# A four-layer hybrid network in one program: where a gated output lives in PSUM, and how the expert stages begin and end

## The reference

```python
# layer 0: deformable convolution (8 groups, 9 taps), batch norm as a scale and a shift, and a gate
out = (acc * mask[..., None]).sum(axis=3).reshape(N, P, C) @ w_out + b_out
out = out * inv + (bn_beta - bn_mean * inv)
x = x + out * sigmoid(out)
# layer 1: a scan layer;  layer 2: attention by cosines, then experts
t = t + experts_2(layernorm(t))
# layer 3: additive attention, then experts
t = t + attention_3(layernorm(t))
t = t + experts_3(layernorm(t))
x = t.transpose(0, 2, 1).reshape(x.shape)          # back to channels

def experts(x):                                    # both expert layers
    probs = softmax(x @ router_w + router_b)
    top_p, top_i = top_k(probs, 2);  top_p = top_p / sum(top_p)
    out = einsum("bnd,edc->bnec", x, expert_w) + expert_b      # 8 experts
    return sum over the two chosen experts of top_p * out
```

## Time and profile before

| what | value |
| --- | --- |
| median of 3 runs | 8086.49 us (8081.16 to 8256.99) |
| profiled execution, its own time | 8087.35 us |
| its span | 8085.6 us |
| busy: TensorE, VectorE, ScalarE, GpSimd | 6444.7, 6521.0, 5476.0, 2058.6 us |
| mean granted clock of TensorE | 0.921 of 2.4 GHz |
| deformable layer | to about 1881 us |
| expert stage L2 | 3518 to about 3826 us |
| expert stage L3 and way out | 7964 to 8065, and 8065 to 8085.6 us |

### The profile page before, as it was taken

The page is one execution under the profiler, slowest core; times in us unless marked ns, Lnnn a source line. Parts: engine busy times, 40 slices in busy tenths (PEclk is TensorE's granted clock), DMA queues, the critical chain, the costliest instruction groups (busy, mean ns, idle before and its releaser), DMA issues. The chain is left out here.

```text
span 8085.6 us, 98492 instructions
## 1 busy us (share of the span) xinstructions
PE 6444.7 (80%) x36662; PEld 2250.5 (28%) x36662; DVE 6521.0 (81%) x12658; ACT 5476.0 (68%) x4096; POOL 2058.6 (25%) x1980
## 2 busy tenths in 40 slices
PE   7988898886888599989677776788767877778777
PEld 2222222222344234434221112222222222222223
DVE  7899899997675577758887778898888898888985
ACT  4223222222555455535899998999989999899995
POOL 5556665661000166546100000000000000000002
PEclk9999999987888799989899998999989999899998
DMA  1000000000100000000000000000000000000000
GB/s 51 1 1 1 1 1 1 1 1 15 28 23 24 8 1 1 1 3 1 6 1 1 1 1 1 1 1 1 1 11 1 1 1 1 11 1 1 1 1 24
DMA packets 19194, 46.19 MB, mean 6 GB/s; under 512 B 5786, under 2 KB 8604, under 8 KB 17566
## 3 DMA queue, kind: packets, MB, share of 16 engines
q1 hardware_dynamic: 18718, 39.86, 1.6%
HBM read 14.68 MB, written 8.39 MB: 3 GB/s over the span
## 5 line engine op out<-in xcount | busy, mean ns | idle before, releaser
L2440 ACT ACTIVATE aa_tanh<-aa_tanh 128x4096 f32<-128x4096 f32 (+8 forms) x1280 | 3686.9, 2963 | 117.9 <-DVE aa_tanh L2617 117.7
L2617 DVE TENSOR_SCALAR aa_tanh<-aa_f_times,aa_g_bias 128x1024 f32<-128x1024 f32 (+18 forms) x5120 | 2982.4, 646 | 593.2 <-PE aa_scores L2485 588.7
L2485 PE MATMUL aa_scores<-aa_tanh,aa_w_spread 128*32 128x512 f32 (+8 forms) x18432 | 2177.6, 587 | 827.1 <-ACT aa_tanh L2440 731.3
L2485 PEld LDWEIGHTS aa_scores<-aa_tanh,aa_w_spread 128*32 128x32 f32 x18432 | 583.5, 112 | 2257.0 <-ACT aa_tanh L2440 1051.1
L278 POOL TENSOR_TENSOR near_tap_weights<-near_hat_y_mask,near_hat_x 128x1024 f32<-128x1024 f32 x400 | 935.9, 2364 | 464.6 <-PE near_weights_spread L562 459.3
L562 PE MATMUL near_weights_spread<-near_tap_weights,near_spread_consts 36*64 36x512 f32 x6272 | 795.0, 626 | 164.2 <-DVE near_weighted L346 156.2
L576 PE MATMUL near_out_sum<-near_weighted,near_w_out 128*128 128x512 f32 x1408 | 735.4, 647 | 77.6 <-DVE near_weighted L357 76.6
L2499 PE MATMUL aa_out_sum<-aa_weights,aa_normed 128*128 128x512 f32 (+3 forms) x1152 | 649.7, 648 | 120.6 <-DVE aa_weights L2626 120.5
L2407 POOL TENSOR_SCALAR aa_group_normed<-x_rows,norm_scale,aa_shift_plus 128x128 f32<-128x128 f32 x96 | 75.3, 796 | 2453.2 <-PE aa_turned L2526 1780.5
L346 DVE TENSOR_TENSOR near_weights_spread<-near_weights_spread,near_values 128x1024 f32<-128x1024 f32 x432 | 529.1, 1225 | 86.2 <-PE near_weights_spread L562 81.3
L357 DVE TENSOR_TENSOR near_weighted<-near_weighted,near_weights_spread 128x1024 f32<-128x1024 f32 x432 | 527.3, 1221 | 20.8 <-DVE near_weights_spread L346 0.5
(11 more groups left out here) (355 smaller groups left out, 7230.5 us busy)
## 6 DMA issues: line engine op xcount, KB each, us to landing
l_taps<-l_scan_in_out SPq DMA_DIRECT2D x256, 64.0 KB, 2.0
x_rows<-in_x SPq DMA_DIRECT2D x4, 2048.0 KB, 14.7
out_x<-x_rows SPq DMA_DIRECT2D x4, 2048.0 KB, 6.3
qa_weights_in<-in_quantum SPq DMA_DIRECT2D x1, 1280.0 KB, 5.8
L_ffn_expert_w<-in_L_ffn_expert_w SPq DMA_DIRECT2D x2, 512.0 KB
near_spread_consts<-in_deform_consts SPq DMA_DIRECT2D x1, 805.5 KB, 7.7
l_weights<-in_mamba SPq DMA_DIRECT2D x1, 557.0 KB
consts_sb<-in_consts SPq DMA_DIRECT2D x1, 516.5 KB
```

The source lines that it names most:

```text
L2440: a.activation(TH[:, (4 * n + tt) % PLACES, 0:length], TH[:, (4 * n + tt) % PLACES, 0:length], ACT.Tanh).then_inc(th_ready, 1)
L2485: last = t.matmul(sp_[32 * q:32 * q + 32, n % 2, s:e], W2S[:, tt, :], TH[:, (4 * n + tt) % PLACES, o + s:o + e], start=tt == 0, stop=tt == ...
L2617: ins = v.tensor_scalar(TH[:, (4 * n + tt) % PLACES, at[q]:at[q] + w - s], FR[:, m % 2, lo + s:CHUNK], GB[:, key:key + 1], None, ALU.add)
```

## The change

1. **Deformable layer.** The gate writes its result back into `acc` in PSUM, and `YB` is no longer used for it. `add_out` reads `acc` and stands after shift 2 of the next block, not after shift 8. TensorE's first sum of the next block waits for that add (`x_done`) and no longer for the gate (`y_ready`); the gate waits for no add.
2. **Expert stages.** VectorE normalizes the first 16 tiles into a tile of its own (`UF`); GpSimd begins with the fifth group. TensorE turns the first four groups, then centres the router, makes all four groups of logits, and then centres the expert weights, which ScalarE copies out in two halves. Seven semaphores more are raised at the start of the stage.
3. **Weights kept.** `attention_and_experts` writes its centred weights to tiles that outlive it, and the last expert stage uses them: no loads and no centring there.
4. **Way out inside.** In the last expert stage finished tiles are turned back inside the loop (`turn_back`, `store_back`), seven groups of four after the tiles 17, 19, 21, 23, 25, 27 and 30 and the last after the loop, through the PSUM places of `turn`; ScalarE stores them and SP sends each group (256 KB) as it is stored. `to_channels` is gone.

```diff
@@ deform_near @@
-                v.tensor_tensor(x, x, YB[:, :, :], ALU.add).then_inc(x_done, 1)
+                v.tensor_tensor(x, x, acc[:, :, :], ALU.add).then_inc(x_done, 1)
...
-                    if U and t == 8:
+                    if U and t == 2:
                         add_out(U - 1)
...
             def bn_gate(U):
                 a.wait_ge(proj, 1 + (U + 1) * NGR)
-                if U:
-                    a.wait_ge(x_done, 1 + U)
-                a.activation(YB[:, :, :], acc[:, :, :], ACT.Silu, bias=BB[:, 0:1], scale=INV[:, 0:1]).then_inc(y_ready, 1)
+                a.activation(acc[:, :, :], acc[:, :, :], ACT.Silu, bias=BB[:, 0:1], scale=INV[:, 0:1]).then_inc(y_ready, 1)
...
                 if g == 0 and U:
-                    t.wait_ge(y_ready, 1 + U)
+                    t.wait_ge(x_done, 1 + U)
@@ moe_layer @@
+        if kept:
+            RWC, EWC = kept
...
+        backs = {}
+        if out is not None:
+            for g in range(NTL // 4 - 1):
+                backs[max(4 * g + 6, NTL - CK + 2 * g + 1)] = g
...
         @block.sync
+            if out is not None:
+                for g in range(NTL // 4):
+                    sp.wait_ge(stored, 1 + g + 1)
+                    sp.dma_start(out[:, g * BANK:(g + 1) * BANK], T[:, first * P + g * BANK:first * P + (g + 1) * BANK]).then_inc(sent, 16)
+                sp.wait_ge(sent, 1 + 16 * (NTL // 4))
+            if kept:
+                return
...
         @block.gpsimd
-            pool.memset(ON[:, :], 1.0 / P).then_inc(prep, 1)
-            pool.wait_ge(prep, 1 + 3)
-            for g in range(CG):
-                normalize(g)
+            if not kept:
+                pool.memset(ON[:, :], 1.0 / P).then_inc(prep, 1)
+            pool.wait_ge(sh_ready, 1 + 1)
...
         @block.tensor
+            def turn_back(g):
+                n = NTL // 4 + g
+                t_.wait_ge(t_ready, 1 + 4 * g + 4)
+                if g >= 2:
+                    t_.wait_ge(stored, 1 + g - 1)
+                for k in range(4):
+                    last = t_.transpose(up[:, n % 2, k * P:(k + 1) * P], tokens(4 * g + k), C["ident"])
+                last.then_inc(back, 1)
...
             for g in range(CG):
                 turn(g)
-                if g:
-                    logits(g - 1)
-            logits(CG - 1)
+            if not kept:
+                t_.wait_ge(loaded, 1 + 64)
+                t_.wait_ge(prep, 1 + 2)
...
+            for g in range(CG):
+                logits(g)
+            if not kept:
...
             for t in range(NTL):
...
+                if t in backs:
+                    turn_back(backs[t])
+            if out is not None:
+                turn_back(NTL // 4 - 1)
...
         @block.scalar
+            def store_back(g):
+                a.wait_ge(back, 1 + g + 1)
+                a.activation(T[:, (first + 4 * g) * P:(first + 4 * g + 4) * P], up[:, (NTL // 4 + g) % 2, :], ACT.Copy).then_inc(stored, 1)
...
+                if t - 1 in backs:
+                    store_back(backs[t - 1])
...
         @block.vector
+            v.tensor_scalar(SH1[:, first:TT], N.shift[:, first:TT], 1.0, None, ALU.add).then_inc(sh_ready, 1)
+            v.wait_ge(sh_ready, 1 + 1)
+            for t in range(CK):
+                ins = v.tensor_scalar(UF[:, t // 4, t % 4 * P:(t % 4 + 1) * P], tokens(t), N.scale[:, first + t:first + t + 1], SH1[:, first + t:first + t + 1], ALU.mult, ALU.add)
+                if t % 4 == 3:
+                    ins.then_inc(first_ready, 1)
@@ build @@
-        moe_layer(nc, d, X, C, N, "L3_ffn_", False, TT - NT)
-        to_channels(nc, X, C, out, NB - 1)
+        moe_layer(nc, d, X, C, N, "L3_ffn_", TT - NT, (RWC, EWC), out.rearrange("b c h w -> b c (h w)")[NB - 1])
```

More of the change, by code:

```diff
@@ L1939, with moe_layer @@
 CG = CK // 4
-def moe_layer(nc, d, T, C, N, tag, last_norm, first=0):
+def moe_layer(nc, d, T, C, N, tag, first=0, kept=None, out=None):
     with stage_semaphores(nc, tag) as sem, ExitStack() as ctx:
@@ L1971, in moe_layer @@
                              "vector_norm", "var", "std"))
+        first_ready, rw_done, rw_ready, sh_ready, back, stored, sent = (sem(n) for n in ("first_normed", "router_done", "router_ready", "shift_ready", "turned_back", "stored", "sent"))
         block = ctx.enter_context(nc.Block())
@@ L2025, in turn @@
             def turn(g):
-                t_.wait_ge(un_ready, 1 + g + 1)
+                if g < CG:
+                    t_.wait_ge(first_ready, 1 + g + 1)
+                else:
+                    t_.wait_ge(un_ready, 1 + g - CG + 1)
                 if g >= 2:
                     t_.wait_ge(ut_ready, 1 + g - 1)
+                src = UF[:, g, :] if g < CG else UN[:, g % 2, :]
                 for k in range(4):
-                    last = t_.transpose(up[:, g % 2, k * P:(k + 1) * P], UN[:, g % 2, k * P:(k + 1) * P], C["ident"])
+                    last = t_.transpose(up[:, g % 2, k * P:(k + 1) * P], src[:, k * P:(k + 1) * P], C["ident"])
                 last.then_inc(turned, 1)
+            def turn_back(g):
[6 more added lines that the diff above has]
+                last.then_inc(back, 1)
             def logits(g):
@@ L2083, in gate_exp @@
                 a.activation(M1[:, :], M2[:, :], ACT.Exp).then_inc(e_ready, 1)
-            a.wait_ge(w_done, 1 + 1)
-            a.activation(EWC[:, 4:8, :].rearrange("p e c -> p (e c)"), ep[:, 0, 1, :], ACT.Copy).then_inc(w_ready, 1)
+            def store_back(g):
+                a.wait_ge(back, 1 + g + 1)
+                a.activation(T[:, (first + 4 * g) * P:(first + 4 * g + 4) * P], up[:, (NTL // 4 + g) % 2, :], ACT.Copy).then_inc(stored, 1)
             for g in range(CG):
                 store(g)
+            if not kept:
+                for h in range(2):
+                    a.wait_ge(w_done, 1 + h + 1)
+                    a.activation(EWC[:, 4 * h:4 * h + 4, :].rearrange("p e c -> p (e c)"), ep[:, 0, h, :], ACT.Copy).then_inc(w_ready, 1)
             gate_exp(0)
@@ L2103, in _ @@
                         gate_exp(c)
-            if last_norm:
+                if t - 1 in backs:
+                    store_back(backs[t - 1])
+            if out is None:
                 N.scalar(a, vv, ss)
+            else:
+                store_back(NTL // 4 - 1)
         @block.vector
@@ L2166, in statistics @@
             def statistics(t):
-                if last_norm:
+                if out is None:
                     v.wait_ge(t_ready, 1 + t + 1)
                     v.bn_stats(N.stats[:, 6 * (first + t):6 * (first + t) + 6], tokens(t)).then_inc(st_ready, 1)
-            v.tensor_scalar(CM[:, :], C["ident"], -1.0 / P, None, ALU.add).then_inc(prep, 1)
-            v.tensor_scalar(SH1[:, :], N.shift[:, :], 1.0, None, ALU.add).then_inc(prep, 1)
-            v.wait_ge(w_done, 1 + 1)
-            v.tensor_copy(RWC[:, :], ep[:, 1, 0, 0:EX]).then_inc(w_ready, 1)
-            v.tensor_copy(EWC[:, 0:4, :].rearrange("p e c -> p (e c)"), ep[:, 0, 0, :]).then_inc(w_ready, 1)
+            v.tensor_scalar(SH1[:, first:TT], N.shift[:, first:TT], 1.0, None, ALU.add).then_inc(sh_ready, 1)
[4 more added lines that the diff above has]
+                    ins.then_inc(first_ready, 1)
+            if not kept:
+                v.tensor_scalar(CM[:, :], C["ident"], -1.0 / P, None, ALU.add).then_inc(prep, 1)
+                v.wait_ge(rw_done, 1 + 1)
+                v.tensor_copy(RWC[:, :], ep[:, 1, 0, 0:EX]).then_inc(rw_ready, 1)
             keep_logits(0)
```

68 lines of the change are left out of this document (19 added, 49 removed).

## The result

The changed kernel takes **7881.57 us** (median of 4 runs, 7869.30 to 7884.39) against 8086.61 us: a ratio of 0.9746, with an interval from 0.9727 to 0.9765. That is 205 us less; the forecast was 232.5 less, 7854 us, and the measured time lies inside the range of 7830 to 7925.

| part | read from | forecast | measured |
| --- | --- | --- | --- |
| deformable layer | last add: 1879.6 before, 1705.3 after | 207 | 174.3 |
| expert stage L2 | its shift tile 174.2 earlier, that of L3 177.3 earlier | 2.5 | 3.1 |
| head of L3 | first expert sum 188.0 earlier (7996.07, 7808.09) | 10 | 10.7 |
| loop of L3 and way out | end 203.0 earlier | 13 | 15.0 |

The account below looks back on a forecast made before the run. The prediction took VectorE to pace the deformable layer, its add waiting for GpSimd, with TensorE then at half clock. Gains of 207 (layer), 10, 13 and 2.5 us (expert stages) sum to 232.5, giving 7854 us, range 7830 to 7925.

Parts of the forecast that it names:

- The add's wait: Deformable layer: the add, 13.73 us behind GpSimd's work, falls to about 1.22; about 181 us net of TensorE's new wait.
- The gate in PSUM at no cost: Deformable layer: the gate writing PSUM costs nothing, with 1.05 us of cover before the add's earliest start.
- The new wait, 1.76 us a block: Deformable layer: TensorE's first output matmul of each block waits 1.76 us for the add, 26 us in all, bounds 0 and 3.
- shifts 0 to 8: Start of each deformable-layer block: 21.97 us afterwards against 33.97 in block 14, 12.0 less.
- The clock: Deformable layer: about 26 us gained because TensorE no longer works at half clock after the add's wait.
- a clock of 0.50 inside blocks: Deformable layer: a sign against the prediction, which expected the granted clock at 1.00 from 200 us to the layer's end.
- shifts 9 to 13: Deformable-layer block, eight operations: 9.76 us without a value piece, 11.4 with one, 13.03 with two.
- The first rival: TensorE's new idle time at block starts lowers the clock, 6.8 us a block, 102 in all: 7956 us; chance 0.12.
- VectorE paces the layer at 1.26 us each: Deformable layer at full clock: shifts 23 to 48, 40 operations, take 50.48 us, unchanged, so VectorE's time counts one to one.
- Second: Rival, deformable layer: the add still waits for GpSimd, TensorE right behind it; 8136 us, +0.6%; chance 0.04.
- third rival: Deformable layer: GpSimd loses its lead and becomes the bound, some 4 us a block: 7914 us; chance 0.04.
- Expert stages: Three gains: 2.5 us in L2, 10 at L3's head by kept weights, 13 in L3's loop and way out.

Follow-up runs that it names:

- run 6: The changed kernel with the gated output in SBUF again, the add still after shift 2: 8064.93 us, ratio 0.9963.
- run 7: The kernel before the change with one more wait: GpSimd holds ahead of class 10's tap weights until the add is done; 7878.68 us, ratio 0.9747.
- run 2: The changed kernel with the add after shift 1 of the next block, not after shift 2: 7850.94 us, ratio 0.9705.
- run 4: The changed kernel with the add after shift 3 of the next block, not after shift 2: 7922.92 us, ratio 0.9795.
- run 3: The changed kernel with TensorE's first output sum of a block issued after the spread of shift 4, not shift 3: 7826.98 us, ratio 0.9677.
- run 5: The changed kernel with every output sum of a block but its last issued one shift later: 7804.28 us, ratio 0.9657.
- run 1: The kernel before the change with only the four edits of the deformable layer, expert stages as before: 7904.34 us, ratio 0.9774.

## Why the prediction was right, and where it was short

- **The add's wait** (main step): right, and shown from both sides, by the operand's memory (run 6) and by the length of GpSimd's run (run 7).
- **The gate in PSUM at no cost**: right, 1.18 us.
- **The new wait, 1.76 us a block**: 1.78, 27.8 us in all. That it counts one to one is shown by runs 2 and 4: where the clock stays up, shifts 0 to 8 are 1.05 us shorter for 1.04 us less of it in run 2, and in run 4 some 2.3 us longer for 2.39 us more, with the low stretch behind it taken off. Run 3 gains 2.5 us for 1.78, since it also puts the sum behind a spread.
- **The clock** ("about 26 for the clock"): this step failed. I had it at full speed from the first add to the layer's end. The prediction named a clock of 0.50 inside blocks as a sign that would make it wrong; that sign came, and blocks 1 to 14 last 101.5 to 106.2 us, not 101 throughout. The low stretches grew short but did not go: 13 of them in blocks 1 to 15, nine after the new stand and four in shifts 14 to 22, some 22 us. In what it costs, the clock gave nothing back: before the change, shifts 9 to 22 of these blocks took some 21 us more than the same shifts take in the changed kernel at the full clock. Most of the low time that went had cost little: shifts 9 to 13 held 139 us of it before, for some 11 us lost. The first rival, that the new wait cools TensorE, came true in 9 of 15 blocks, but at 1.4 to 1.7 us each (2.3 in block 1, part of it because the stand there is 1.1 us longer) and not at 6.8: I had priced it with a block that is low for most of its first half, and a single stand brings one short stretch. Its evidence against, a clock of 1.00 beside idle TensorE from 3549 to 3552, was one look at a thing that happens in some cases only.
- **Terms of the sum that were too small**: shifts 0 to 8 without a low stretch are 22.3 and not 21.97 (about 5 us in all); shifts 9 to 13 with one value piece take 11.75 to 12.4 and not 11.4, the middle I had chosen between two rows (6 us). In both TensorE is the busier engine (block 3: 19.57 of 22.31 and 11.24 of 12.07 us, VectorE 17.84 and 9.63). With the 22 of the clock these are the 33 us, but for half a microsecond in shifts 23 to 48.
- **"VectorE paces the layer at 1.26 us each"**: only nearly. Run 5 shows 49.75 us in place of 50.5 for the same VectorE work.
- **Second and third rival**: neither occurred. In the changed kernel no instruction of VectorE in the layer waits for GpSimd, which speaks against the third. The second, with the long add standing before TensorE, needs an add of two SBUF operands; run 6 has one, 15.1 us long, though TensorE does not wait for it there, and the layer loses all of its gain.
- **Expert stages**: 28.8 us measured and 25.5 forecast. The sixteen normalizations took 4.19 and not 3.3, and the last group was stored 0.5 us later than forecast; but TensorE had begun the logits of the first groups 0.8 us before that, which the forecast had one after the other, and the first sum came 0.4 us sooner (18.2 for 18.6). Here two errors offset each other; the loop lost 1.6 us to the turns, not 3.5, as the last finished rows show (186.4 us earlier with the stage's first sum 188.0 earlier); the tail gained 16.6 (16.3).

What stays open: why some stands of the same length are followed by the low clock and others aren't, and so how many blocks are hit in one execution. An add from PSUM after shift 8, as the other half of run 6, wasn't tried: TensorE's next sums need the same PSUM banks, and all of them are in use.

## What to carry to other kernels

A VectorE operation of two SBUF operands beside a busy GpSimd is priced by GpSimd's unbroken run, not by its own length; one operand in PSUM, or a single wait that breaks the run at the right place, takes most of that wait away, and here the single wait gained the more of the two, since it made no other engine stand. After such a stall is gone, ask which engine stands next and for how long: a stand of TensorE costs its length and, in some cases, a short stretch at half clock behind it, and issuing the waiting matmul one step later, behind work that is ready, removed both at the blocks' starts (run 3). A stretch built from rows of two engines at full load wants the slower engine's own sum beside it.

## What the runs showed of the hardware

- The stand that goes ahead of a fall of the clock can be short. One of 4.17 us was followed by a fall in 15 of 15 cases (run 4), one of 1.78 us in 8 of 14 (the changed kernel; the ninth, in block 1, is of 2.85 us) and in 7 of 14 (run 1), one of 0.74 us in 0 of 14 (run 2). Stands of 0.96 to 1.32 us for the add L357 were followed by one in 16 of 365 (the changed kernel and runs 1 to 4). In run 5 one of the 57 stands of 0.52 us was, in block 1, and one of the four of 0.70 to 1.03 after block 1; with so few falls these rates can't be told from 16 of 365.
- VectorE's add of two SBUF operands waits for several GpSimd instructions in a row (15.1 us in the median of run 6, 17.4 at most), and for the present one alone (2.2 us) where GpSimd then stops (run 7).
- 256 KB land in 2.0 us, as 64 KB do.
